# A fused attention and FP4 FFN layer on eight cores: own buffers for the first keys and values, another order of exponentials and statistics, x tiles ahead of the last chunks

## The chip, the cores and the metric

The kernel runs on the 8 cores of one Trainium2 chip. Each core takes two sequences of 2048 tokens out of sixteen and works alone; the weights are prepared on every core. The metric is the device time of the slowest core in microseconds. A core has TensorE (matmuls), VectorE, ScalarE, GpSimd (Pool) and SyncE (SP), each with its own instruction queue, done strictly in order; engines wait for each other through semaphores. DMAs are issued from the queues of ScalarE, Pool and SP.

## The reference

```python
xn = layernorm(x)                                  # rows of 1024
x = x + attention(xn) + ffn(xn)

# attention: 16 heads of 64, per sequence
q, k, v = split(xn @ Wqkv + bqkv)
# queries come in the order of a fixed mapping; every block of 64 queries
# sees 64 keys, each fourth of its segment of 256, also through the mapping
p = exp(q_block @ k_sel.T * D**-0.5 - rowmax)
out = (p @ v_sel) / (1e-6 + p.sum(-1)) @ Wproj + bproj

# ffn: weights [2816, 1024] twice and [1024, 2816]; xn, h and the weights go
# through fp4 (blocks of 16 along the last dimension, scale = max|.| / 6)
h = silu(fp4(xn) @ fp4(w_gate).T) * (fp4(xn) @ fp4(w_up).T)
ffn = fp4(h) @ fp4(w_down).T
```

## The kernel before

There are two blocks with a barrier between them. The first makes the attention part and, beside it, quantizes the FFN weights. The second is the FFN over 32 row tiles, and is not touched.

In the first block the FFN weights are cut into chunks of 128 rows: 24 of `wd` (stored to `wd_dram`), 22 of `wg`, 22 of `wu` (transposed by DMA into `wgqT` and `wuqT`), and two row tiles of x, which are normalized and quantized for the FFN. Each chunk c goes through a slot of VectorE (`slot(c)`: block maxima L746, scale and reciprocal L752 and L755, product L758; and for chunk c - 1 the rounding L749 and the last product L761) and a pass of ScalarE (`w_pass(c)`: L556 and L561, between the product and the rounding, then the load of chunk c + 2). SP stores or transposes the result (`w_store`). The buffers `wrow`, `wki` and `wcl` are double, so a chunk's load, pass and store each bound the chunk two further on.

`PRO` chunks belong to the prologue, which also loads the attention weights, gathers rows of x, makes the keys (`k_blocks`, four of two banks) and values (`v_rows`, four) of the first sequence, stores them to `k_dram` and `v_dram`, and makes the first queries. Keys go through one buffer `kst`, half of them at a time, and values through one buffer `vst`, a quarter at a time. Both alias or stand beside `wuqT`. The rows of x are handled in pieces of 128 rows: gathered by Pool into `lnx` (three buffers) or `lnk`, statistics by VectorE for two pieces at a time (`ln_batch`), normalized by ScalarE (`ln_apply`), turned by TensorE (`turn_piece`, L400) and copied out by ScalarE (`piece_evac`, L591).

Then there are 32 tiles J of 128 queries. `quota` says how many chunk slots a tile has, one or two; `TAIL` slots follow the last tile. In a tile TensorE turns the piece or pieces of `turned_at(J)`, projects the attention output of tile J - 2 (`proj`), makes the first half of the scores of J + 1, half a pair of queries (`q_half`), the second half of the scores, in tiles 5 to 12 a key or value block of the second sequence (`kv_at`), turns the output of J - 1, and multiplies with the values (`pv`). All results but scores and `pv` go through a ring of three PSUM banks `psR` in the order written out in `order`. VectorE takes the maxima of the scores (`colmax`, L786 and L791), does its slots and `norm(J - 1)` (L796 to L806). ScalarE makes the exponentials (`exps`, L645), copies out projections, queries, keys and values, the turned output (`at_evac`, L596), and does its passes.

Of VectorE's order in a tile before, these lines matter:

```python
colmax(J)
for i in batches_at(J): ln_batch(i)     # for turned_at(J + 1)
for c in slots[0:1]: slot(c)
if J >= 1: norm(J - 1)
for c in slots[1:]: slot(c)
```

## Time and profile before

| what | value |
|---|---|
| time, median of 3 runs | 1665.97 us (1660.42 to 1845.73) |
| profiled execution | 1663.18 us |
| its span, slowest core (core 5) | 1661.5 us |
| spans of the 8 cores | 1646.2 to 1661.5 us |
| busy of the span: TensorE, VectorE, ScalarE, Pool | 85%, 78%, 57%, 11% |
| mean granted clock of TensorE, core 5 | 0.928 of full |

The rows further below are of core 5, times in us from its first instruction. An idle time in square brackets is that of the engine just before the instruction, with what ended it. L numbers are lines of the kernel before. The first block ends near 735 us.

### The profile page before, as it was taken

How to read it: one execution, taken by the hardware profiler on the slowest of the kernel's cores; microseconds unless marked ns; L12 is line 12 of the kernel's file. 1: busy time of each engine (PE TensorE's matmuls, PEld its weight loads, DVE VectorE, ACT ScalarE, POOL GpSimd, SP SyncE). 2: the span in 40 equal slices, each digit the busy share in tenths (PEclk: the TensorE clock that was granted, in tenths of full speed). 3: DMA queues.
4: the chain of work that ended last, by engine and by line, in shares of the span. 5: the costliest groups of instructions: out<-in, count | busy, mean ns of one | idle time of the engine just before them, and what ended most of it. 6: DMA issues, size and time to landing. Idle time of an engine off the chain costs nothing.

```text
span 1661.5 us, 27839 instructions; the slowest of 8 cores (1646.2 to 1661.5 us)
## 1 busy us (share of the span) xinstructions
PE 1405.2 (85%) x8976; PEld 731.0 (44%) x8976; DVE 1287.9 (78%) x2251; ACT 941.1 (57%) x1594; POOL 181.9 (11%) x202
## 2 busy tenths in 40 slices
PE   0455788887777678649999999999999999999997
PEld 0224454454444445314444444444444444444443
DVE  3538876667877888848988888888888888888855
ACT  1436886677767777535555555545455555555542
POOL 4112212221221212000000000000000000000000
PEclk9978788999787778779999999999999999999999
DMA  7985455565777669884445454555555454545353
GB/s 157 212 215 175 142 152 156 166 157 169 184 163 188 170 149 180 177 184 93 92 120 121 102 105 108 108 108 109 115 106 119 96 128 97 103 110 111 90 105 90
DMA packets 252784, 225.68 MB, mean 136 GB/s; under 512 B 202914, under 2 KB 208034, under 8 KB 252642
## 3 DMA queue, kind: packets, MB, share of 16 engines
q1 hardware_dynamic: 213026, 103.91, 28.3%
q0 software_dynamic: 19616, 63.33, 18.4%
q10 hardware_dynamic: 20000, 56.66, 11.4%
q8 instruction: 74, 1.21, 0.3%
q14 instruction: 68, 0.56, 0.1%
HBM read 139.68 MB, written 43.81 MB: 110 GB/s over the span
## 4 chain that ended last, share of the span: by engine, by line
PE 52%; DVE 1%; DMA 1%; issue 1%; ACT 0%; DVEq 0%; SPq 0%; ACTq 0%
PE psD L1000 18%; PE psG L978 17%; PE psV L985 17%; DMA hqT<-wc 1%; DMA xb<-xin 0%; DVE sg L1081 0%; DVE wc L1102 0%; DVE am L1086 0%; DVE rs L1096 0%; DVE st_bn L122 0%; ACT xb L1041 0%; DVE xam L1064 0%; DVE st_bn L123 0%; DVE st_u L137 0%; DVE st_u L135 0%
## 5 line engine op out<-in xcount | busy, mean ns | idle before, releaser
L978 PE MATMUL psG<-wgqT,xq 128*128 128x512 bf16 (+1 forms) x1536 | 337.2, 363 | 17.4 <-PEq L268 17.4
L985 PE MATMUL psV<-wuqT,xq 128*128 128x512 bf16 (+1 forms) x1536 | 335.8, 362 | 0.0
L1000 PE MATMUL psD<-wdqT,hqT 128*128 128x512 bf16 x1408 | 316.7, 381 | 4.7 <-DMA hqT<-wc 4.7
L978 PEld LDWEIGHTS psG<-wgqT,xq 128*128 128x128 bf16 x1536 | 150.6, 98 | 178.8 <-issue 19.3
L985 PEld LDWEIGHTS psV<-wuqT,xq 128*128 128x128 bf16 x1536 | 150.4, 98 | 154.4 <-issue 0.8
L1000 PEld LDWEIGHTS psD<-wdqT,hqT 128*128 128x128 bf16 x1408 | 138.3, 98 | 166.8 <-issue 9.1
L1036 ACT COPY su<-psV 128x512 f32<-128x512 f32 (+1 forms) x192 | 105.7, 551 | 181.3 <-PE psV L985 181.2
L1032 ACT ACTIVATE sg<-psG 128x512 f32<-128x512 f32 (+1 forms) x192 | 107.8, 561 | 172.3 <-PE psG L978 172.2
L491 PE MATMUL psR<-wdqT,atT 128*128 128x512 bf16 x512 | 164.0, 478 | 11.9 <-ACT atT L596 11.8
L400 PE MATMUL psR<-ident,wdqT 128*128 128x128 bf16 x320 | 35.6, 281 | 154.0 <-ACT wdqT L572 95.0
L962 POOL DMA_DIRECT2D pp<-xin x32 | 28.0, 874 | 952.6 <-DMA pp<-partial_dram 952.3
L444 PE MATMUL psR<-wdqT 128*128 128x256 bf16 x1024 | 121.1, 278 | 7.6 <-ACT QT L635 3.0
L1014 ACT ACTIVATE ki<-sg 128x1408 int16<-128x1408 f32 x64 | 87.9, 1373 | 69.8 <-DVE sg L1099 69.8
L645 ACT ACTIVATE E<-psS,nb 128x64 bf16<-128x64 f32 x512 | 108.3, 370 | 2.4 <-DVE nb L791 2.4
L444 PEld LDWEIGHTS psR<-wdqT 128*128 128x128 bf16 x1024 | 99.4, 100 | 22.4 <-issue 8.4
L1099 DVE TENSOR_TENSOR sg<-sg,rs 128x1408 f32<-128x1408 f32 x64 | 104.0, 1625 | 6.7
L1086 DVE TENSOR_REDUCE am<-sg 128x88 f32<-128x1408 f32 x64 | 103.7, 1620 | 6.6
L1081 DVE TENSOR_TENSOR sg<-sg,su 128x1408 f32<-128x1408 f32 x64 | 103.8, 1622 | 2.5 <-ACT su L1036 1.7
L746 DVE TENSOR_REDUCE wam<-wrow 128x64 f32<-128x1024 f32 (+1 forms) x70 | 83.0, 1186 | 28.4 <-DMA wrow<-wd 21.6
L1102 DVE TENSOR_TENSOR wc<-wc,hsc 128x1408 bf16<-128x1408 f16 x64 | 103.5, 1618 | 0.1
L556 ACT ACTIVATE wki<-wrow 128x1024 int16<-128x1024 f32 (+1 forms) x70 | 72.3, 1034 | 54.2 <-DVE wrow L758 39.8
L749 DVE TENSOR_SCALAR wcl<-wcl 128x1024 uint16<-128x1024 uint16 (+1 forms) x70 | 29.1, 415 | 92.6 <-ACT wcl L561 92.3
(108 smaller groups left out, 1855.8 us busy)
## 6 DMA issues: line engine op xcount, KB each, us to landing
partial_dram<-po ACTq DMA_DIRECT2D x32, 512.0 KB
pp<-partial_dram SPq DMA_DIRECT2D x32, 512.0 KB, 4.7
pp<-xin POOLq DMA_DIRECT2D x32, 512.0 KB, 5.7
out<-pp SPq DMA_DIRECT2D x32, 512.0 KB, 5.4
xb<-xin SPq DMA_DIRECT2D x30, 512.0 KB, 5.2
wrow<-wg ACTq DMA_DIRECT2D x22, 512.0 KB
wrow<-wu ACTq DMA_DIRECT2D x22, 512.0 KB
wrow<-wd ACTq DMA_DIRECT2D x16, 512.0 KB
```

Of the source, the lines that this page charges most:

```text
L444: mm = tensor.matmul(ps[:, 256 * a:256 * (a + 1)], Wq[:, k, 128 * (2 * b + a):128 * (2 * b + a + 1)], src[:, k, :], start=(k == 0), stop=( ...
L491: tensor.matmul(ps[:], atT[:, k, :], Wproj_sb[:, k, 512 * oc:512 * (oc + 1)], start=(k == 0), stop=False)
L645: ev = scal.activation(E[J % 2][:, 64 * h:64 * (h + 1)], psS[:, 64 * h:64 * (h + 1)], AF.Exp, scale=SCALE, bias=nb_s[J % 2][:, h:h + 1])
L978: m = tensor.matmul(psG[g % 3][:, 0:iw], xqT[t % 2][:, k, :], wgqT[:, k, HU * half + i0:HU * half + i0 + iw], start=(k == 0), stop=(k == N ...
L985: m = tensor.matmul(psV[g % 3][:, 0:iw], xqT[t % 2][:, k, :], wuqT[:, k, HU * half + i0:HU * half + i0 + iw], start=(k == 0), stop=(k == N ...
L1000: m = tensor.matmul(psD[oc][:], hqT[u % 3][:, k, :], wdqT[:, HB * half + k, 512 * oc:512 * (oc + 1)], start=(half == 0 and k == 0), stop=( ...
L1032: silu_ev.inc(scal.activation(sg[s % 2][:, i0:i0 + iw], psG[g % 3][:, 0:iw], AF.Silu))
L1036: copy_ev.inc(scal.copy(su[s % 2][:, i0:i0 + iw], psV[g % 3][:, 0:iw]))
L1081: h_mul.inc(vec.tensor_mul(h, h, su[u % 2][:]))
L1086: h_am.inc(vec.tensor_reduce(am[u % 2][:], blocks(h), AX.X, ALU.max, apply_absolute_value=True))
L1099: h_v.inc(vec.tensor_tensor(blocks(h), blocks(h), spread(rs[u % 2][:], NB), ALU.mult))
L1102: h_out.inc(vec.tensor_tensor(blocks(w), blocks(w.bitcast(F16)), spread(sc[b % 2][:], NB), ALU.mult))
```

## The change

- `kst0` and `vst0`, in parts of `wgqT` that no chunk has reached yet, hold all keys and all values of the first sequence. Its keys are stored in one DMA of 1 MB after the fourth key block, in place of two halves; its four value blocks wait for no store. The second sequence has the small buffers as before. The counts of `kvst` follow, and SP waits for the first sequence's stores before the first gate chunk.
- ScalarE's prologue: passes 4 to 11 come earlier among the key, value and query copies; passes 12 to 14 are added. `PRO` is 15 in place of 12; tiles 14, 16 and 18 have one slot in place of two.
- ScalarE's tile begins with `exps(J)`; then the pieces are copied out, then the first pass, then `proj_evac`, and `ln_apply` for the next tile's pieces stands right behind it in place of at the tile's end.
- VectorE's statistics for `turned_at(J + 2)` stand at the end of tile J; before, those for `turned_at(J + 1)` stood behind `colmax(J)`. The batch of `turned_at(1)` goes into the prologue.
- The two x tiles are chunks 63 and 64, ahead of the last five of `wu`; they were the last two. Their statistics are called from within `slot`. With them the early transposes for `wdqT` begin one tile sooner (two in each of tiles 29, 30 and 31, then one behind each of two tail slots).

```diff
+        kst0 = normed[:, 8192:12288].rearrange("p (s a k) -> p s a k", a=8, k=64)
+        vst0 = normed[:, 12288:12288 + 4 * VW].rearrange("p (g h c) -> p g h c", g=4, c=65)
...
-            FIRST_GATE, FIRST_UP, FIRST_X = 3 * NKC, 3 * NKC + NIC, 3 * NKC + 2 * NIC
-            for r in range(2):
-                chunks.append((xin, xqT[r][:, :, :], r, 0, D))
+            FIRST_GATE, FIRST_UP = 3 * NKC, 3 * NKC + NIC
+            FIRST_X = FIRST_UP + NIC - 5
+            chunks[FIRST_X:FIRST_X] = [(xin, xqT[r][:, :, :], r, 0, D) for r in range(2)]
-            PRO = 12
+            PRO = 15
-            quota = [1 if J in (1, 2, 3, 4, 6, 8, 10, 12) else 2 for J in range(NJ)]
+            quota = [1 if J in (1, 2, 3, 4, 6, 8, 10, 12, 14, 16, 18) else 2 for J in range(NJ)]
...
                         if c == FIRST_GATE:
                             sync.wait_ge(ln_xn.h, kpiece(1, 3) + 1)
+                            sync.wait_ge(kvst.h, 16 * 5)
...
-                        if J >= NJ - 2:
-                            for r in range(2 * (J - NJ + 2), 2 * (J - NJ + 3)):
+                        if J >= NJ - 3:
+                            for r in range(2 * (J - NJ + 3), 2 * (J - NJ + 4)):
                                 wd_early(r)
...
                     def k_evac(q, b):
-                        if b % 2 == 0 and 6 * q + b // 2:
-                            scal.wait_ge(kvst.h, 16 * (6 * q + b // 2))
+                        if q == 1 and b == 2:
+                            scal.wait_ge(kvst.h, 16 * 6)
...
+                        if q == 0 and b == 3:
+                            scal.wait_ge(r_free.h, n + 2)
+                            scal.dma_start(out=k_dram[0][:, :].rearrange("(s p) c -> p s c", p=128),
+                                           in_=kst0.rearrange("p s a k -> p s (a k)")).then_inc(kvst.h, 16)
...
                     k_evac(0, 0)
+                    w_pass(4)
                     k_evac(0, 1)
-                    w_pass(4)
                     k_evac(0, 2)
+                    w_pass(5)
                     k_evac(0, 3)
-                    w_pass(5)
                     piece_evac(qpiece(0))
                     piece_evac(qpiece(1))
                     ln_apply(qpiece(2))
                     ln_apply(qpiece(3))
+                    w_pass(6)
                     v_evac(0, 0)
                     v_evac(0, 1)
-                    w_pass(6)
+                    w_pass(7)
                     v_evac(0, 2)
                     v_evac(0, 3)
-                    w_pass(7)
+                    w_pass(8)
...
                     for J in range(NJ + 2):
                         slots = slots_of(J)
+                        if J < NJ:
+                            exps(J)
                         for key in turned_at(J):
                             piece_evac(pieces.index(key))
-                        if J < NJ:
-                            exps(J)
+                        for c in slots[0:1]:
+                            w_pass(c)
                         if 0 <= J - 2 < NJ - 1:
                             proj_evac(J - 2)
-                        for c in slots[0:1]:
-                            w_pass(c)
+                        for key in turned_at(J + 1):
+                            ln_apply(pieces.index(key))
...
-                        for key in turned_at(J + 1):
-                            ln_apply(pieces.index(key))
...
-                            if c >= FIRST_X:
+                            if FIRST_X <= c < FIRST_X + 2:
+                                x_stats(c)
                                 vec.wait_ge(w_n.h, c - FIRST_X + 1)
...
+                    for i in batches_at(1):
+                        ln_batch(i)
                     for J in range(NJ + 1):
                         slots = slots_of(J)
                         if J < NJ:
                             colmax(J)
-                        for i in batches_at(J):
-                            ln_batch(i)
                         for c in slots[0:1]:
                             slot(c)
                         if J >= 1:
                             norm(J - 1)
                         for c in slots[1:]:
                             slot(c)
+                        for i in batches_at(J + 2):
+                            ln_batch(i)
```

`batches_at(J)` is now written for `turned_at(J)`. `w_pass(c)` ends, as before, with the load of chunk c + 2 and, ahead of an x tile, with its normalization (`x_norm(c + 1)`), which waits for VectorE's statistics.

## Rows read from the trace of the kernel before

**Rows 1.** Windows by stage: length, busy us (instructions) by engine, TensorE's clock, DMA share, GB/s.

```profile
0.00:151.40 151.40, 54.67 (x344) 29.74 (x344) 74.37 (x170) 56.84 (x71) 44.81 (x60) 0.93 0.85 198
...
227.10:374.70 147.60, 125.59 (x1159) 73.98 (x1156) 96.78 (x209) 104.74 (x240) 32.18 (x32) 0.91 0.57 156
374.70:486.65 111.95, 82.49 (x838) 51.28 (x836) 87.81 (x174) 80.22 (x178) 23.85 (x24) 0.85 0.67 175
486.65:612.60 125.95, 92.21 (x910) 57.12 (x910) 100.16 (x196) 91.92 (x204) 26.29 (x27) 0.78 0.68 168
612.60:702.20 89.60, 68.38 (x622) 38.61 (x623) 76.48 (x134) 64.55 (x154) 11.66 (x12) 0.77 0.85 178
...
735.00:1661.50 926.50, 917.38 (x4480) 439.25 (x4480) 772.00 (x1172) 472.26 (x603) 27.96 (x32) 0.99 0.50 108
```

**Rows 2.** Waits of VectorE, 152 to 728 us: total, times, longest.

```profile
DVE wcl L749 <- ACT wcl L561: 63.3, 15, 8.8
DVE mx L786 <- PE psS L465: 14.5, 7, 3.6
```

**Rows 3.** Timeline of VectorE, tiles 19 and 20.

```profile
486.65 1.22 DVE L786 TENSOR_REDUCE mx<-psS 128x16 f32<-128x1024 f32 x1
...
492.85 0.29 DVE L796 TENSOR_SCALAR ls<-psP 128x6 f32<-128x6 f32 x3
...
495.12 1.21 DVE L746 TENSOR_REDUCE wam<-wrow 128x64 f32<-128x1024 f32 x1
500.64 0.43 DVE L749 TENSOR_SCALAR wcl<-wcl 128x1024 uint16<-128x1024 uint16 x1 [4.31 <-ACT wcl L561]
...
504.20 1.22 DVE L786 TENSOR_REDUCE mx<-psS 128x16 f32<-128x1024 f32 x1
...
523.38 1.22 DVE L786 TENSOR_REDUCE mx<-psS 128x16 f32<-128x1024 f32 x1
```

**Rows 4.** Timeline of ScalarE, tile 19.

```profile
487.87 1.23 ACT L572 ACTIVATE wdqT<-lnx,row_n,row_r 128x1024 bf16<-128x1024 f32 x1
490.45 1.01 ACT L591 COPY wdqT<-psR 128x1024 bf16<-128x1024 bf16 x1 [1.36 <-PE psR L400]
491.36 3.38 ACT L645 ACTIVATE E<-psS,nb 128x64 bf16<-128x64 f32 x16
...
499.48 1.06 ACT L561 ACTIVATE wcl<-wki 128x1024 f16<-128x1024 int16 x1
```

**Rows 5.** Timeline of ScalarE in the prologue.

```profile
78.59 0.39 ACTq L610 DMA_DIRECT2D k_dram<-wuqT  x1
...
100.25 1.84 ACT L605 ACTIVATE wuqT<-psR,bqk 128x512 bf16<-128x512 f32 x3 [18.90 <-DMA k_dram<-wuqT]
```

**Rows 6.** DMA queues (packets, MB, share), 85 to 90 us, then 104 to 108.

```profile
q0 software_dynamic: 362, 0.66, 87.8%
q10 hardware_dynamic: 364, 0.19, 17.3%
...
q0 software_dynamic: 218, 0.76, 49.5%
```

**Rows 7.** Timeline of VectorE in the prologue.

```profile
103.39 1.22 DVE L746 TENSOR_REDUCE wam<-wrow 128x64 f32<-128x1024 f32 x1 [12.78 <-DMA wrow<-wd]
...
140.66 1.22 DVE L746 TENSOR_REDUCE wam<-wrow 128x64 f32<-128x1024 f32 x1 [1.73 <-DMA wrow<-wd]
...
151.36 1.22 DVE L786 TENSOR_REDUCE mx<-psS 128x16 f32<-128x1024 f32 x1
```

**Rows 8.** Timeline of VectorE, tiles 7 and 8.

```profile
279.25 0.43 DVE L749 TENSOR_SCALAR wcl<-wcl 128x1024 uint16<-128x1024 uint16 x1 [8.83 <-ACT wcl L561]
...
298.56 1.23 DVE L786 TENSOR_REDUCE mx<-psS 128x16 f32<-128x1024 f32 x1 [1.95 <-PE psS L465]
```

**Rows 9.** The tail: timeline of VectorE, then of SP's queue.

```profile
726.81 1.22 DVE L761 TENSOR_TENSOR wcl<-wcl,wsc 128x1024 bf16<-128x1024 f16 x1
...
730.81 1.36 SPq L285 DMA_TRANSPOSE xq<-wcl x1
```

More of the change, by code:

```diff
@@ L97, in build_nc @@
         kxT = early[:, 16384:20480].rearrange("p (k t) -> p k t", t=512)
-        kst = early[:, 20480:22528].rearrange("p (s a k) -> p s a k", a=4, k=64)
+        kst1 = early[:, 20480:22528].rearrange("p (s a k) -> p s a k", a=4, k=64)
         normed = wgqT[:].rearrange("p k n -> p (k n)")
+        kst0 = normed[:, 8192:12288].rearrange("p (s a k) -> p s a k", a=8, k=64)
+        vst0 = normed[:, 12288:12288 + 4 * VW].rearrange("p (g h c) -> p g h c", g=4, c=65)
         lnk = [normed[:, 2048 * i:2048 * (i + 1)].bitcast(F32) for i in range(4)]
@@ L311, in _ @@
                         if i < 2:
-                            wd_early(4 + 2 * i)
-                            wd_early(5 + 2 * i)
+                            wd_early(6 + i)
                     sync.wait_ge(wdl_early.h, 16 * NKC)
@@ L337, in gather_kv @@
                         if j == 0:
-                            gpsimd.wait_ge(kvst.h, 16 * 6 * (q + 1))
+                            gpsimd.wait_ge(kvst.h, 16 * (5 + 6 * q))
                         if J >= 3:
@@ L366, in _ @@
                     gpsimd.memset(vst[:, :, 64:65], 1.0).then_inc(ones_done.h, 1)
+                    gpsimd.memset(vst0[:, :, :, 64:65], 1.0).then_inc(ones_done.h, 1)
                     for n in range(3, 5):
@@ L564, in w_pass @@
                             w_load(c + 2)
-                        if FIRST_X <= c + 1 < NCH:
+                        if FIRST_X <= c + 1 < FIRST_X + 2:
                             x_norm(c + 1)
@@ L615, in v_evac @@
                         if q == 0 and g == 0:
-                            scal.wait_ge(ones_done.h, 1)
-                        else:
-                            scal.wait_ge(kvst.h, 16 * (6 * q + 2 + g) if g else 16 * 6)
+                            scal.wait_ge(ones_done.h, 2)
+                        if q == 1 and g >= 1:
+                            scal.wait_ge(kvst.h, 16 * (5 + 2 + g))
+                        dst = vst0[:, g] if q == 0 else vst[:]
                         for oc in range(2):
                             scal.wait_ge(r_full.h, n + oc + 1)
-                            scal.copy(vst[:, 8 * oc:8 * (oc + 1), 0:64],
+                            scal.copy(dst[:, 8 * oc:8 * (oc + 1), 0:64],
                                       psR[(n + oc) % 3][:].rearrange("p (h d) -> p h d", d=64)).then_inc(r_free.h, 1)
@@ L691, in _ @@
                     ln_apply(qpiece(5))
-                    w_pass(8)
+                    w_pass(9)
                     q_evac(0, 0)
-                    w_pass(9)
+                    w_pass(10)
                     q_evac(0, 1)
-                    w_pass(10)
+                    w_pass(11)
                     q_evac(1, 0)
                     piece_evac(qpiece(4))
-                    w_pass(11)
+                    for c in range(12, PRO):
+                        w_pass(c)
                     for J in range(NJ + 2):
                         slots = slots_of(J)
+                        if J < NJ:
+                            exps(J)
                         for key in turned_at(J):
                             piece_evac(pieces.index(key))
-                        if J < NJ:
-                            exps(J)
+                        for c in slots[0:1]:
+                            w_pass(c)
                         if 0 <= J - 2 < NJ - 1:
                             proj_evac(J - 2)
-                        for c in slots[0:1]:
-                            w_pass(c)
+                        for key in turned_at(J + 1):
+                            ln_apply(pieces.index(key))
                         if q_step(J)[0] < NJ // 2:
@@ L780, in x_stats @@
                         xs_nm.inc(row_stats(vec, [wrow[c % 2][:]], 3, row_r[:, r:r + 1], row_n[:, r:r + 1]))
-                    batches_at = lambda J: [m // 2 for m in map(pieces.index, turned_at(J + 1)) if m % 2 == 0]
+                    batches_at = lambda J: [m // 2 for m in map(pieces.index, turned_at(J)) if m % 2 == 0]
                     def colmax(J):
```

15 lines of the change are left out of this document (7 added, 8 removed).

## The prediction

> **What bounds the kernel now.** I read the windows by stage first [rows 1]. From 735 us on the FFN runs with TensorE busy 917 of 926.5 us, and nothing of the change is in that block, so those 926.5 us stay. The 735 us before it are where the change acts, and no engine is full there: VectorE is the nearest. So I read what VectorE waits for [rows 2]: in the tile loop it stands 63.3 us, 15 times, before the rounding step on `wcl` (L749) because ScalarE has not made `wcl` yet, and 14.5 us, 7 times, before colmax for the scores. Then I read one pair of tiles in order of time [rows 3]. Tile 20 (504.20 to 523.38) takes 19.18 us with no wait: it has two chunk slots and a batch of row statistics. Tile 19 (486.65 to 504.20) has two slots, no batch, takes 17.55 us and holds a wait of 4.31 us. So its work is 13.24 us, the batch costs 19.18 - 13.24 = 5.9, and from the rows inside tile 19 (495.12 to 504.20 less 4.31) one slot costs 4.8, norm 2.3. The reason of the wait stands in ScalarE's rows of tile 19 [rows 4]: it normalizes the piece at 487.87, waits for TensorE to turn it, copies it out at 490.45, only then begins the exponentials (491.36), and the first chunk's pass ends at 500.5; the pass was computable long before. In the prologue the same reading gives one large hole: ScalarE stands 18.90 us before the third key block for the store of the first [rows 5], and VectorE 12.78 us for chunk 6 [rows 7]. The tail is VectorE's last product, then SP issuing the last transpose at 730.81 [rows 9].
>
> **The prologue.** Own buffers `kst0` and `vst0` remove the 18.90 us wait and the one for the vector store behind it. What is late next? ScalarE now meets `w_pass(6)` ahead of the value blocks, and that needs chunk 6. Its load was queued behind the key store on ScalarE's ring. In 85 to 90 us that ring and the software queue each got through some 70 packets per us, 364 against 362 [rows 6]: one for one. The store is 1024 packets, so it took its 21 us because of their number. After the change the loads of chunks 6 and 7 (128 packets each) are issued before the store (all eight blocks must be copied first, I work out 86 us), so chunk 6 lands near 85, not 103.4; then the store's 1024 packets of twice the size take 15 to 20 us and hold back chunk 8 to about 104. VectorE's batch 4 then needs a row gather that Pool issues once ScalarE has normalized piece 2 (near 92, before 111); it stands in the software queue, which is running out at 104 to 108 [rows 6]: I take 108. From there VectorE has batch 4 (5.9), seven slots (8 to 14, before four) at the 5.35 us a slot of the last two before (140.66 to 151.36 [rows 7]), which already holds the waits for loads, and batch 5, which stood behind colmax before: 108 + 5.9 + 37.5 + 5.9 = 157.3 against 151.4. So tile 0 begins 6 us later, with three chunks and a batch more behind it: 20 us of VectorE work for 6. Bounds: -2 (the gather lands at 100) and +12 (chunk 6 lands no earlier than before, so slot 8 starts near 120). I take +6, since the packet rows are of this very queue. The one more memset on Pool is under 1 us in a queue that waits for loads anyway.
>
> The Trainium skill (DMA: Bandwidth & Descriptors, "Queues, rings and completion order") says that each DMA engine takes turns between its rings a packet at a time; the 364 to 362 agree, and by it chunk 6 lands early. The same page ("Issuing engines are not separate DMA queues") speaks against a gain: all queues share the same 16 engines. By that alone chunk 6 would come when the software queue empties; that is the +12 end, and the first rival.
>
> **Tiles 0 to 4** (75.7 us, between the first two stages [rows 1]). The batch of tile J now stands at the end of J - 1, ahead of the next colmax; four batches lie here, before five: -5.9. Tile 4 is then short of VectorE work and goes by ScalarE and the scores: +3.7 from the colmax waits, which run from 0.2 to 3.6 us [rows 2]. Sum -2 (bounds -6, +3).
>
> **Tiles 5 to 12** (147.6 us, 18.45 a tile). Here the second sequence's keys and values are made. VectorE is busy 96.8 us of them, so the batch is covered; the 8.83 us wait [rows 8] is ScalarE's lateness again. TensorE has 125.6 us, 15.7 a tile [rows 1], ScalarE 13.1. In the new order TensorE turns the piece and projects while ScalarE still does the previous tile, the copy follows the exponentials without the 1.36 us wait [rows 4]. What is late next is the ring of three banks: q's second bank needs the first projection copied out. I give 1.4 us a tile for that on top of TensorE's 15.7: 17.1 x 8 = 137, -11. Bounds: 15.9 a tile (-20), and 18.45 (0).
>
> **Tiles 13 to 18** (112.0 us). Quota is now one slot in 14, 16 and 18. VectorE's pair was 13.24 + 19.18 = 32.4, now less one slot 27.6. In the one-slot tile colmax comes early and waits for scores: I add 2.6 (2.1 on average [rows 2]). ScalarE: exponentials 3.15, copy 0.9, pass 2.2 after nb; VectorE needs the pass 9 us after nb (slot 4.8, norm 2.3, half a reduce), so the 4 us wait is gone with 2 us to spare. 3 x 30.2 = 90.7, +3 for matmuls at the lower clock (granted 0.85 here): 94, -18. Bounds -24 (27.6 a pair and the clock kept) and -10 (half the wait stays).
>
> **Tiles 19 to 25** (126.0 us). Same chunks as before; only the waits go. Three pairs at 32.4 and one tile of 13.24: 110.5. Where no batch stands between two slots, a load has some 7 us from issue to need, and the DMA engines are 0.68 busy: I add 3 for that. 113.5, -12. Bounds -15 and -3 (the waits stay, as loads).
>
> **Tiles 26 to 31 and the tail** (122.4 us to 735). One wait of this kind falls away (-3). The two x tiles go from the tail into tiles 29 and 30, with their statistics, ScalarE's normalization and the wait for it: the same VectorE work. ScalarE stands in `x_norm` behind `w_pass(62)` and `w_pass(63)` until VectorE has come to the statistics; queued behind are `proj_evac`, `at_evac` and once `exps(30)`; VectorE needs none of them before its next two slots, so this costs nothing here, and up to 5 if it does. The tail is now three plain slots, but with DMA 0.85 busy the loads get no pause: +6. SP's last transpose no longer stands behind two early ones for `wd` (728.03 to 730.81 [rows 9]): -3. Those early transposes start one tile sooner, behind conditions that hold by tile 29. Sum 0 (bounds -8, +8).
>
> **The sum.** +6 - 2 - 11 - 18 - 12 + 0 = -37. The profiled execution took 1663.2 us (span 1661.5 and 1.7 around it), so 1626; the median of the runs stands 2.8 us above it, and I predict 1628 us, 2.3% under 1666. A measurement of this kernel tells about 2% from no change, that is 1633: the forecast is near that edge.
>
> **Rivals.** (1) DMA takes the bound. For: 0.85 busy in 612 to 702, and 0.67 to 0.68 in 375 to 612 with less done per us than wanted now; VectorE's waits turn from ScalarE into loads and `wcl` transposes. Against: only two load waits in the loop, both late. Price: the prologue at +12, and 2 us in each of the 14 tiles 13 to 26, which is half the gain: -37 + 6 + 20 = -11, 1655.
> (2) The store wait was worth all of its 19 us: the gather lands by 100 and colmax(0) is at 149, and tiles 5 to 12 go at TensorE's own 15.9: -37 - 8 - 9 = -54, 1611. For: the engines were idle, not busy, at 85 to 100. Against: seven chunk slots are a chain of loads that nothing shortens.
> (3) The other side: TensorE becomes the bound at its lower clock. It has two levels, 1.2 and 2.4 GHz, and was granted 0.91 in tiles 5 to 12 and 0.78 to 0.85 behind them [rows 1]. The new order makes it wait for the exponentials between projection and scores, in the middle of its work. A tile of 5 to 12 needs about 16 us at full clock, the others 11.7. If 0.91 fell to 0.70, the eight tiles would take 22.9 each, +35 in place of -11, and the others 16.7 for 16.2, +10: -37 + 46 + 10 = +19, 1685. It decides from a mean grant below 0.75 there. Against: total idle of TensorE shrinks as the tiles shorten.
> (4) The change does less than it says: the order frees ScalarE, but the late pass is only exchanged for a late projection copy and late scores: half of tiles 13 to 25: -37 + 15 = -22, 1644.
>
> **Chances.** Forecast 0.50 (own range 1615 to 1640; 0.37 of it under 1633), (1) 0.18, (2) 0.13, (3) 0.08, (4) 0.11. Faster by over 2%: 0.37 + 0.13 = 0.50; slower by over 2%, that is past 1699: 0.03 of (3) and 0.03 of (1), where both grow past what I price: 0.06; within: 0.44. The range for 8 in 10 reaches from (2)'s upper half to (1): 1608 to 1656.
>
> **What would show it.** Right: no wait of ScalarE for `k_dram`; chunk 6 landed by 90; colmax(0) at 152 to 163; the L749 waits in the loop from 63 to under 15 us; pairs near 32.4 us in 19 to 24 and 30 in 13 to 18; no projection or turn of TensorE behind `ln_apply`. Wrong: if colmax(0) is past 165, if VectorE waits for `wrow` or ScalarE for transposes of `wcl` over 20 us in the loop, or if the granted clock in tiles 5 to 12 is under 0.8.

## The result, and the profile after

| | median of the runs | ratio to before |
|---|---|---|
| before | 1665.97 us | |
| after | 1639.71 us (4 runs, 1636.45 to 1783.88 us) | 0.9852, 95% interval 0.9804 to 0.9901 |
| forecast | 1628 us (1608 to 1656) | 0.977 |

The kernel is faster by 1.5%, within the 2% that a measurement of it can tell from no change. The profiled execution took 1640.51 us, 22.7 us less than before's, and the slowest core is now core 3 with a span of 1638.7 us. Runs in which the cores of one die ran at a lower clock count in the medians of this table and are left out of every ratio and of the medians further below; without them the two medians are 1663.20 and 1638.91 us.

The windows by stage of core 3 of the kernel after, to be held against [rows 1]; columns are start and end, length, busy us (instructions) of TensorE, its weight loads, VectorE, ScalarE and Pool, then TensorE's granted clock, DMA share and GB/s:

```profile
0.00:174.25 174.25, 58.92 (x344) 31.52 (x344) 91.94 (x203) 64.01 (x78) 42.58 (x61) 0.85 0.80 190
...
252.43:382.27 129.84, 117.87 (x1159) 70.32 (x1157) 97.77 (x209) 102.93 (x237) 30.24 (x31) 0.99 0.61 178
382.27:481.64 99.37, 78.86 (x814) 49.98 (x813) 74.28 (x157) 73.91 (x174) 24.77 (x25) 0.88 0.72 174
481.64:592.40 110.76, 84.43 (x938) 55.10 (x935) 99.92 (x195) 88.58 (x202) 26.07 (x25) 0.91 0.68 184
592.40:682.00 89.60, 60.21 (x580) 34.56 (x576) 76.79 (x153) 63.92 (x153) 13.51 (x12) 0.81 0.76 169
...
708.93:1638.70 929.77, 918.84 (x4480) 439.54 (x4480) 772.59 (x1172) 473.12 (x603) 27.69 (x32) 0.99 0.50 108
```

The windows are the prologue, tiles 5 to 12, 13 to 18, 19 to 25, the 89.6 us from tile 26 on (as in [rows 1]) and the FFN. The first has grown from 151.4 to 174.25 us; tiles 5 to 12, 13 to 18 and 19 to 25 take 129.84, 99.37 and 110.76 us in place of 147.60, 111.95 and 125.95. Since the slowest core is another one than before, I took the stages of all eight cores from the timelines (the first colmax, the colmax of tiles 5, 13, 19 and 26, the first matmul of the FFN) and use their means from here on:

| stage, mean of 8 cores, us | before | after | difference | forecast |
|---|---|---|---|---|
| prologue, to colmax(0) | 149.6 | 172.0 | +22.4 | +6 |
| tiles 0 to 4 | 75.4 | 75.7 | +0.3 | -2 |
| tiles 5 to 12 | 146.8 | 130.0 | -16.8 | -11 |
| tiles 13 to 18 | 110.5 | 97.9 | -12.6 | -18 |
| tiles 19 to 25 | 124.5 | 110.2 | -14.3 | -12 |
| tile 26 to the FFN | 120.2 | 115.6 | -4.6 | 0 |
| first block | 727.0 | 701.3 | -25.7 | -37 |

From tile 0 on the loop gave 48 us where 43 were forecast. The prologue took 22 back where 6 were forecast, and that is the miss. The FFN, which the change does not touch, took 927.8 us in the mean of the cores and 925.9 before.

**The prologue.** VectorE's timeline of the kernel after, core 3 (compare [rows 7]; the third batch of statistics, the fourth, and the first colmax):

```profile
85.75 0.70 DVE L124 BATCH_NORM_STATS2 st_bn<-xq 128x6 f32<-128x512 f32 x1 [4.06 <-DMA lnx<-xin,qidx]
...
122.56 0.70 DVE L124 BATCH_NORM_STATS2 st_bn<-lnx 128x6 f32<-128x512 f32 x1 [21.60 <-DMA xq<-xin,qidx]
...
174.25 1.23 DVE L798 TENSOR_REDUCE mx<-psS 128x16 f32<-128x1024 f32 x1
```

The same batch in VectorE's timeline of the kernel before, core 5:

```profile
124.96 0.69 DVE L122 BATCH_NORM_STATS2 st_bn<-lnx 128x6 f32<-128x512 f32 x1
```

Batch 4 waits 21.60 us for a gather and starts at 122.56; before it started at 124.96, with no wait ahead of it. Removing ScalarE's 18.90 us wait [rows 5] moved that batch by 2.4 us (from 123.7 to 122.0 in the mean of the eight cores). Pool's timeline of the kernel after, core 3, shows why:

```profile
76.32 4.36 POOL L373 DMA_DIRECT2D wdqT<-Wproj  x8
...
85.28 0.94 POOL L328 DMA_INDIRECT wgqT<-xin,kidx  x1 [0.27 <-issue]
93.60 0.93 POOL L334 DMA_INDIRECT xq<-xin,qidx  x1 [7.38 <-ACT wdqT L575]
...
136.70 0.94 POOL L334 DMA_INDIRECT lnx<-xin,qidx  x1 [40.96 <-ACT wdqT L575]
```

And Pool's timeline of the kernel before, core 5:

```profile
111.28 0.94 POOL L332 DMA_INDIRECT xq<-xin,qidx  x1 [24.10 <-ACT wdqT L572]
```

The gather is issued at 93.60, before at 111.28: 18 us earlier, as the change intends. But it lands at 122. It stands in the software queue behind the eight loads of `Wproj` and four gathers of keys, and that queue is served more slowly while ScalarE's ring has packets. The DMA queues of the kernel after, core 3 (packets, MB, share), 100 to 105 us, then 120 to 125:

```profile
q0 software_dynamic: 352, 0.98, 74.4%
q10 hardware_dynamic: 355, 0.36, 21.3%
...
q10 hardware_dynamic: 310, 0.70, 35.5%
q0 software_dynamic: 63, 0.21, 10.3%
```

352 packets of the one for 355 of the other. Before, ScalarE waited for the first key store until 99.74 us on this core, had put nothing behind it but one load, and issued the next store only at 105.00; so its ring was nearly empty from 100 to 105. The same window of core 3 before:

```profile
q0 software_dynamic: 458, 1.61, 86.3%
q10 hardware_dynamic: 40, 0.11, 8.0%
```

1.61 MB of the software queue against 0.98. From 85 to 100 the two queues had gone one for one before too; it is above all the ring left empty at the end of the wait that let the software queue run out. From 80 to 105 us that queue moved 4.23 MB before and 3.30 after, and 0.63 of the 0.93 MB between them belong to these 5 us. After 105 it had 0.22 MB left before, and after the change 2.35, of which the two gathers are 1.05 (2 x 128 rows of 4 KB). Nor is a gather done when the backlog is: before, with the queue empty, the same one took 5.2 us from its issue to its landing (core 3).

**The loop.** VectorE's waits from 176 to 705 us on core 3 of the kernel after, to be held against [rows 2] (total, times, longest):

```profile
DVE mx L798 <- PE psS L468: 37.5, 9, 8.1
DVE wcl L761 <- ACT wcl L564: 18.1, 10, 3.1
```

The wait for ScalarE's pass fell from 63.3 us (core 5) to 18.1 (core 3) and 20.7 (core 5). The wait of colmax for the scores rose from 14.5 to 37.5 and 29.2. VectorE's timeline in tiles 14 to 17, then in tiles 20 to 22 (compare [rows 3]):

```profile
404.83 1.22 DVE L798 TENSOR_REDUCE mx<-psS 128x16 f32<-128x1024 f32 x1
...
417.25 1.23 DVE L798 TENSOR_REDUCE mx<-psS 128x16 f32<-128x1024 f32 x1 [3.85 <-PE psS L468]
...
436.48 1.22 DVE L798 TENSOR_REDUCE mx<-psS 128x16 f32<-128x1024 f32 x1
...
449.74 1.23 DVE L798 TENSOR_REDUCE mx<-psS 128x16 f32<-128x1024 f32 x1 [4.69 <-PE psS L468]
...
500.44 1.23 DVE L798 TENSOR_REDUCE mx<-psS 128x16 f32<-128x1024 f32 x1
...
513.61 1.22 DVE L798 TENSOR_REDUCE mx<-psS 128x16 f32<-128x1024 f32 x1
...
533.22 1.23 DVE L798 TENSOR_REDUCE mx<-psS 128x16 f32<-128x1024 f32 x1
```

Tiles 20 and 21 take 533.22 - 500.44 = 32.8 us with no wait ahead of a colmax, against the 32.4 worked out. Tiles 14 and 16, with one slot, end in waits of 3.85 and 4.69 us: a slot that is taken out there is mostly waited out.

**The tail.** VectorE's timeline, then SP's queue, of the kernel after on core 3, compare [rows 9]:

```profile
703.66 0.43 DVE L761 TENSOR_SCALAR wcl<-wcl 128x1024 uint16<-128x1024 uint16 x1 [2.97 <-ACT wcl L564]
704.20 1.23 DVE L773 TENSOR_TENSOR wcl<-wcl,wsc 128x1024 bf16<-128x1024 f16 x1
...
705.49 1.22 SPq L288 DMA_TRANSPOSE wuqT<-wcl  x1
```

SP issues the last transpose 0.06 us after the last product has ended (704.20 + 1.23 = 705.43); before, 2.8 us after.

### The profile page after: what moved, and what is told of

Its sections match the earlier page's. It is cut to its first block, busy times and chain, and to the rows that moved or that the text cites. A ratio compares the mean times of both kernels' runs of the same rounds, so it can differ in the third digit from the quotient of the medians.

```text
span 1638.7 us, 27833 instructions; the slowest of 8 cores (1617.1 to 1638.7 us)
## 1 busy us (share of the span) xinstructions
PE 1390.1 (85%) x8976; PEld 725.3 (44%) x8976; DVE 1288.3 (79%) x2251; ACT 936.9 (57%) x1594; POOL 182.4 (11%) x203
## 4 chain that ended last, share of the span: by engine, by line
PE 53%; SPq 1%; DVE 1%; DMA 1%; issue 1%; DVEq 0%; ACT 0%; ACTq 0%
PE psD L1012 18%; PE psG L990 17%; PE psV L997 17%; SPq L952 1%; DMA hqT<-wc 0%; DMA xb<-xin 0%; DVE sg L1093 0%; DVE wc L1114 0%; DVE rs L1108 0%; DVE am L1098 0%; SPq L932 0%; DVE st_bn L124 0%; DVE pp L1064 0%; DVE st_bn L125 0%; DVEq L928 0%
## 5 line engine op out<-in xcount | busy, mean ns | idle before, releaser
L447 PE MATMUL psR<-wdqT 128*128 128x256 bf16 x1024 | 146.3, 308 | 66.0 <-ACT wdqT L594 46.7
L447 PEld LDWEIGHTS psR<-wdqT 128*128 128x128 bf16 x1024 | 109.0, 110 | 97.1 <-issue 73.1
L494 PE MATMUL psR<-wdqT,atT 128*128 128x512 bf16 x512 | 130.5, 401 | 16.8 <-ACT atT L599 9.1
L1111 DVE TENSOR_TENSOR sg<-sg,rs 128x1408 f32<-128x1408 f32 x64 | 104.1, 1626 | 6.7
L559 ACT ACTIVATE wki<-wrow 128x1024 int16<-128x1024 f32 (+1 forms) x70 | 76.4, 1092 | 39.2 <-DVE wrow L770 35.7
L1034 ACT ACTIVATE wc<-ki 128x1408 f16<-128x1408 int16 x64 | 87.6, 1369 | 5.2 <-ACT ki L1026 0.4
L770 DVE TENSOR_TENSOR wrow<-wrow,wrs 128x1024 f32<-128x1024 f32 (+1 forms) x70 | 83.7, 1196 | 7.7 <-DVE wrs L767 0.5
```

Of the source, the lines that this page charges most:

```text
L447: mm = tensor.matmul(ps[:, 256 * a:256 * (a + 1)], Wq[:, k, 128 * (2 * b + a):128 * (2 * b + a + 1)], src[:, k, :], start=(k == 0), stop=( ...
L494: tensor.matmul(ps[:], atT[:, k, :], Wproj_sb[:, k, 512 * oc:512 * (oc + 1)], start=(k == 0), stop=False)
L1111: h_v.inc(vec.tensor_tensor(blocks(h), blocks(h), spread(rs[u % 2][:], NB), ALU.mult))
```

## The experiments

Each puts one part of the change (or two) on the kernel before, or changes one to three things in the kernel after. Stages are means over the 8 cores, in us, read as in the table above.

| kernel | median us | ratio, 95% | colmax(0) | 0 to 4 | 5 to 12 | 13 to 18 | 19 to 25 | 26 to FFN |
|---|---|---|---|---|---|---|---|---|
| e1_loop_only | 1624.85 | 0.9739, 0.9690 to 0.9789 | 155.4 | 74.7 | 130.8 | 100.6 | 111.1 | 116.9 |
| e2_prologue_only | 1670.16 | 1.0012, 0.9975 to 1.0049 | 164.7 | 75.9 | 147.7 | 99.8 | 124.7 | 118.9 |
| e3_gather_first | 1637.65 | 0.9801, 0.9739 to 0.9864 | 162.8 | 76.1 | 130.5 | 98.8 | 110.4 | 119.4 |
| e4_two_k_stores | 1649.71, one run | | 173.0 | 75.0 | 130.7 | 98.1 | 110.7 | 117.6 |
| e5_pro12 | 1632.69 | 0.9811, 0.9771 to 0.9851 | 154.6 | 76.0 | 130.6 | 100.7 | 111.3 | 118.2 |
| e6_pro12_gather_first | 1619.11 | 0.9709, 0.9665 to 0.9753 | 146.0 | 75.7 | 131.0 | 100.7 | 111.2 | 117.1 |
| e7_scalar_order_only | 1621.27 | 0.9737, 0.9692 to 0.9782 | 150.4 | 79.3 | 127.1 | 100.6 | 111.0 | 116.2 |
| e8_vector_order_only | 1663.14 | 0.9990, 0.9966 to 1.0013 | 157.4 | 69.8 | 147.0 | 110.5 | 123.9 | 119.2 |
| e9_gather_first_vector_old | 1621.18 | 0.9736, 0.9712 to 0.9760 | 145.2 | 79.0 | 127.1 | 101.9 | 111.4 | 117.1 |
| e10_own_buffers_vector_old | 1625.78 | 0.9764, 0.9733 to 0.9795 | 153.0 | 79.1 | 127.0 | 100.8 | 111.2 | 115.0 |
| e11_scalar_order_early_x | 1629.92 and 1623.01 | | 153.8 | 79.6 | 127.3 | 100.8 | 111.2 | 117.4 |
| e12_scalar_order_gather_first | 1621.27 | 0.9750, 0.9722 to 0.9778 | 151.8 | 79.5 | 127.0 | 101.9 | 110.9 | 116.0 |

### e1_loop_only: the tile order of both engines on the kernel before

```diff
 # ScalarE, tile J
+                        if J < NJ:
+                            exps(J)
                         for key in turned_at(J):
                             piece_evac(pieces.index(key))
-                        if J < NJ:
-                            exps(J)
...
 # VectorE: ln_batch of turned_at(1) ahead of tile 0, of turned_at(J + 2) at the end of tile J
```

> The kernel before with only the new order inside the tiles (exponentials first, statistics at the end of a tile and two tiles ahead, one batch before tile 0); prologue, buffers, quota, chunks and x tiles as before. Theory: all of the gain comes from here. Tile 0 begins one batch (5.9 us) later than before, near 155.5 (mean of the cores), and from there to the FFN it takes 577 - 48 + 14 = 543 us, since the three slots of tiles 14, 16 and 18 are in the loop again. FFN at 699 and about 1637 us, ratio 0.983, as good as the whole change. Rival: the loop is shorter mainly because three slots and a batch were taken out of it; then it is here about 577 - 20 - 8 = 560 us and the ratio 0.993.

It gave 0.9739, more than either theory expected and more than the whole change. With the old prologue the loop takes 534.1 us from colmax(0) to the FFN (529.4 after, 577.4 before). So the prologue of the change costs more than its shorter quota returns.

### e2_prologue_only: own buffers, new prologue order, PRO 15 and the shorter quota, with the old tile order and the x tiles last

```diff
-            PRO = 12
+            PRO = 15
-            quota = [1 if J in (1, 2, 3, 4, 6, 8, 10, 12) else 2 for J in range(NJ)]
+            quota = [1 if J in (1, 2, 3, 4, 6, 8, 10, 12, 14, 16, 18) else 2 for J in range(NJ)]
...
+                        if q == 0 and b == 3:
+                            scal.dma_start(out=k_dram[0][:, :].rearrange("(s p) c -> p s c", p=128),
```

> The change without the new order in the tiles and with the x tiles at the end: own buffers, new order of the prologue, PRO 15, quota. Theory: tile 0 begins at 172 - 6 = 166 us, 16 later than before; in the loop three slots of 4.7 us are gone, 14 us at most, so the whole is 1.00 to 1.01. Rival (the buffers and the earlier chunks pay, the loop order is a small thing): under 0.99.

1.0012: nothing. The prologue is 15.1 us longer, tiles 13 to 18 are 10.7 shorter. With the old order a slot less in tiles 14, 16 and 18 is worth 3.6 us each; with the new order (after against e1) it is worth 2.7 us for the three. The two parts of the change do not add, and VectorE's waits in tiles 13 to 18 (summed from the timelines, mean of the 8 cores) say why. Here the wait for ScalarE's pass is 16.0 us (before 13.4): it stays, and each slot taken out saves most of its work. In the kernel after the pass wait is 3.1, but colmax waits 11.6 for the scores (e1 0.3): a slot taken out is waited out.

### e3_gather_first: the kernel after, with the gathers of pieces 5 and 6 ahead of `Wproj` and the key gathers in Pool's queue

```diff
+                    for n in range(5, 7):
+                        gather_q(n)
                     for k in range(NKC):
                         gpsimd.dma_start(out=Wproj_sb[:, k, :], ...)
...
-                    for n in range(5, 8):
+                    for n in range(7, 8):
                         gather_q(n)
```

> The changed kernel, but Pool issues the gathers of pieces 5 and 6 before the loads of Wproj and the four gathers of key rows, not after them. Theory: batch 4 waits (20 to 22 us in the trace) because the gather of piece 5 lies in the software queue behind 2 x 4 MB of other traffic, which takes turns with ScalarE's ring; with nothing ahead of it it lands near 102 instead of 122, batch 4 begins there, slots 8 to 14 run at 5.4 each, tile 0 begins near 152 to 156 in place of 172; 1622 us, ratio 0.974. Rival: tile 0 is late by three slots and one batch (22 us) because the slots are a chain of loads and passes; then it stays at 168 to 172 and the ratio at 0.985.

VectorE's timeline on core 4 of this kernel: the first instruction of batch 4, then the waits behind it.

```profile
100.95 0.69 DVE L124 BATCH_NORM_STATS2 st_bn<-lnx 128x6 f32<-128x512 f32 x1
...
116.12 1.22 DVE L760 TENSOR_REDUCE wam<-wrow 128x64 f32<-128x1024 f32 x1 [5.50 <-DMA wrow<-wd]
124.79 1.22 DVE L760 TENSOR_REDUCE wam<-wrow 128x64 f32<-128x1024 f32 x1 [4.22 <-issue]
133.19 0.95 DVE L760 TENSOR_REDUCE wam<-wrow 128x48 f32<-128x768 f32 x1 [3.62 <-DMA wrow<-wd]
143.44 1.22 DVE L760 TENSOR_REDUCE wam<-wrow 128x64 f32<-128x1024 f32 x1 [6.11 <-DMA wrow<-wd]
```

The gather wait is gone and batch 4 starts 22 us earlier (99.7 for 122.0 in the mean), so the place in the software queue was its cause. But tile 0 came only 9 us earlier, not the 16 to 20 expected. The next slots stand 19.5 us before a chunk's block maxima: 5.50 + 3.62 + 6.11 for chunk loads, and 4.22 for which the trace names no releaser. From batch 4 to colmax(0) it is now 63.1 us. So the gather was only the last of the late transfers; that they are all late because they share the DMA engines is likely, and not shown apart. Nearly 6 of the 9 us are lost again behind tile 0 (535.2 us to the FFN, 529.4 after), and the whole, 0.9801, is not told apart from the kernel after (the intervals overlap).

### e4_two_k_stores: the kernel after, its key store made twice

```diff
+                            scal.dma_start(out=k_dram[1][:, :].rearrange("(s p) c -> p s c", p=128),
+                                           in_=kst0.rearrange("p s a k -> p s (a k)")).then_inc(kx2.h, 16)
```

The second sequence's keys wait for that store and overwrite it later.

> The changed kernel with the first sequence's key store issued twice on ScalarE's ring, the second time into the other sequence's buffer in DRAM, which is overwritten later (results as before). 1024 packets more. If rings take turns packet by packet, the 1024 packets delay the software queue's by as many: the gather of piece 5 lands about 10 to 15 us later (near 134) and tile 0 begins there, near 184. If only the bytes count (1 MB at 220 GB/s), 5 us: tile 0 near 177. If the gather does not set tile 0, it stays at 172.

Neither delay came: colmax(0) stayed at 173.0 (172.0 without), and batch 4 began at 123.45 behind 19.58 us of wait for the gather (core 4), so the gather was not late either. That is the number of the third branch, but not its reason. The ring was never empty between 96 and 124 us in the kernel after, so the added packets only lengthened ScalarE's own queue and took no more turns from the software queue. So this run tests neither branch: that the ring's packets slow the software queue is read from the packet counts of both kernels, and no run took packets off the ring while the queue had its backlog. What the added packets did was hold ScalarE: issuing one load, elsewhere some 0.3 us, took 12.35 (ScalarE's queue, core 4 of this kernel).

```profile
99.13 12.35 ACTq L547 DMA_DIRECT2D wrow<-wd  x1
```

### e5_pro12 and e6_pro12_gather_first: the kernels after and e3 with PRO 12 and the old quota

```diff
-            PRO = 15
+            PRO = 12
-            quota = [1 if J in (1, 2, 3, 4, 6, 8, 10, 12, 14, 16, 18) else 2 for J in range(NJ)]
+            quota = [1 if J in (1, 2, 3, 4, 6, 8, 10, 12) else 2 for J in range(NJ)]
```

> The whole change but with PRO 12 and the quota of before: own buffers, new prologue order, new tile order, early x tiles. Theory (three prologue slots cost their full 16 us because the prologue is a chain, and give back only 2.7 us in tiles 13 to 18): tile 0 begins near 172 - 16 = 156, the loop takes 529 + 3 = 532, FFN at 688 to 690, 1626 us, ratio 0.974, equal to the kernel with the tile order alone (0.9739). Rival (the three slots fill idle time in the prologue, since VectorE waits 20 us there for a gather): tile 0 stays past 165 and the ratio stays near 0.985.

> As the run before, with the gathers of pieces 5 and 6 ahead of the Wproj loads and the key gathers. Theory: gather order and slot chain add up: tile 0 at 156 - 9 = 147, FFN at 679, 1617 us, ratio 0.968. Rival: with twelve prologue chunks the first queries or the key and value gathers for tile 0 (they need piece 4) become the late thing, and tile 0 stays at 152 or later; 1622 us or more.

e5 came out at 0.9811 where 0.974 was expected; its interval does not reach there. Its stages say what the three slots are worth: 172.0 - 154.6 = 17.4 us in the prologue, 5.8 a slot, against 100.7 - 97.9 = 2.8 in tiles 13 to 18. In e5 batch 4 still starts at 124.14 behind a wait of 21.29 us (core 0). e6 does what was expected, 0.9709 and colmax(0) at 146.0: the early gather is worth 8.6 us here too (9.2 with 15 chunks).

### e7_scalar_order_only and e8_vector_order_only: each engine's tile order alone on the kernel before

```diff
 # e7: ScalarE, tile J
+                        if J < NJ:
+                            exps(J)
                         for key in turned_at(J):
                             piece_evac(pieces.index(key))
-                        if J < NJ:
-                            exps(J)
+                        for c in slots[0:1]:
+                            w_pass(c)
                         if 0 <= J - 2 < NJ - 1:
                             proj_evac(J - 2)
-                        for c in slots[0:1]:
-                            w_pass(c)
+                        for key in turned_at(J + 1):
+                            ln_apply(pieces.index(key))
...
-                        for key in turned_at(J + 1):
-                            ln_apply(pieces.index(key))
 # e8: VectorE only, ln_batch as in e1
```

> The kernel before with only ScalarE's new order in a tile (exponentials first, ln_apply behind the projection copy); VectorE's statistics stay right behind colmax, for one tile ahead. Theory: the 63 us of waits at L749 were made by ScalarE's order alone. Tile 0 at 149.6 as before, the loop 535 to 545 in place of 577, FFN at 685 to 695, ratio 0.972 to 0.979. Rival: both moves are needed, since ln_apply in the middle of a tile now meets statistics that are only just made; then 560 and more, 0.99.

> The kernel before with only VectorE's new order (statistics at the end of a tile, two tiles ahead); ScalarE as before. Theory: the L749 waits stay, the batch only changes sides of colmax; tile 0 at 155.5, the loop 570 to 583, ratio 0.998 to 1.007. Rival (VectorE's move is what matters): 0.985 or less.

Both as the theory had it: 0.9737 and 0.9990. The whole gain of the change is in the order of ScalarE. VectorE's waits from 156 to 700 us, core 1 of e7:

```profile
DVE wcl L749 <- ACT wcl L561: 18.0, 12, 3.1
DVE mx L786 <- PE psS L465: 17.8, 9, 3.0
```

The pass wait is at the value of the whole change, 18.0 us for 18.1. e8's tile order takes 69.8 us in tiles 0 to 4 in place of 75.4, and gives it back ahead of them (157.4 in place of 149.6): a batch is moved, and a moved batch saves nothing.

### e9 to e12: what is left of the other parts

e9 is e6, and e10 is e5, with VectorE's statistics in the old place. e11 is e7 with the x tiles ahead of the last five chunks. e12 is e7 with the two gathers first in Pool's queue.

```diff
 # e9, e10
-                    for i in batches_at(1):
-                        ln_batch(i)
...
                             colmax(J)
+                        for i in batches_at(J):
+                            ln_batch(i)
...
-                        for i in batches_at(J + 2):
-                            ln_batch(i)
 # e11
+            FIRST_X = FIRST_UP + NIC - 5
+            chunks[FIRST_X:FIRST_X] = [(xin, xqT[r][:, :, :], r, 0, D) for r in range(2)]
 # e12: the same lines as e3
```

> PRO 12 with own buffers, ScalarE's new order, x tiles early and the two gathers first (1620.0 us), with VectorE's statistics back in the old place. Theory (a batch of statistics ahead of tile 0 is paid in the prologue, 5.9 us, and its place in the loop is worth nothing): tile 0 at 140 to 142 us in place of 146.0, the loop from tile 0 to the FFN 534 to 537 as with ScalarE's order alone (534.2), so 1614 us, ratio 0.969. Rival (chunk loads set the end of the prologue, since VectorE waits 13.5 us for them behind that batch, so the batch fills a wait): tile 0 stays at 145 to 147, 1620 us, ratio 0.972.

> The kernel of the change with PRO 12 and the old quota, and VectorE's statistics in the old place: own buffers, ScalarE's new order and the early x tiles, the gathers where they were. Theory (the late gather holds tile 0 through batch 4, which now stands behind tile 0): tile 0 at 147 to 149 us, 1622 us, ratio 0.973. Rival (own buffers bring a gain of their own, 19 us of ScalarE's wait, once nothing waits for the gather): tile 0 at 140 or before, ratio 0.967. Second rival (loads of chunks are what is late, with or without the gather): tile 0 at 150 to 155, ratio 0.976 or more.

> The kernel before with ScalarE's new order (1621.6 us, 0.9737) and the x tiles ahead of the last five chunks, nothing else. Theory (the move of the x tiles is worth -2 to +2 us): 0.9725 to 0.975, the stretch from tile 26 to the FFN 114 to 118 us (116.2 without). Rival (it shortens the tail as two transposes fewer stand before the last one): 112 us or less, 0.971. Other rival (ScalarE stands in the x tiles' normalization with exponentials behind it): 121 us or more, 0.977.

> The kernel before with ScalarE's new order, and the two gathers ahead of the projection weights and the second sequence's key rows; no own buffers, so ScalarE still waits 18 us for the key store. Theory (own buffers and the early gathers work only together: without own buffers piece 2 is normalized at 111 us and the gathers cannot be issued earlier): tile 0 at 149 to 152 as without (150.4), ratio 0.974; the weights that now stand behind the gathers are not needed before tile 2. Rival (the early gathers are the whole of the 8.6 us that they brought with own buffers): tile 0 at 142, ratio 0.969.

e9 went to its rival: colmax(0) at 145.2, 1621.18 us. But the batch did not fill a wait for loads, as that rival had it: without it VectorE waits for the scores, 5.7 to 13.7 us on the eight cores, here core 1 of e9:

```profile
148.04 1.23 DVE L800 TENSOR_REDUCE mx<-psS 128x16 f32<-128x1024 f32 x1 [10.99 <-PE psS L470]
```

e10 came out at 153.0 and 0.9764. It has the late gather in batch 4 (core 2: 124.38 behind 23.04 us of wait): batch 4 stands ahead of tile 0 in both orders, the one that VectorE's new order adds ahead of tile 0 is batch 5, and its expectation mixed them up. The number falls under its second rival, though on four cores colmax(0) stands 6.0 to 8.8 us for the scores and not for a load. e11 has only the two times of the table, too few for a ratio; its last stage, 117.4 against e7's 116.2, shows no gain from the x tiles. Its colmax(0) at 153.8 against e7's 150.4, with the same prologue, suggests that colmax(0) moves by some 3 us from one execution to the next; smaller differences of it are not told apart.

e12 is the most telling. Its time is e7's (1621.27 us both), as its theory had it, but not for the theory's reason: ScalarE does not wait 18 us for the key store any more, and the gathers are issued at 97.55, not at 111. ScalarE's timeline, and the DMA queues from 80 to 85 us, core 1 of e12:

```profile
79.35 0.39 ACTq L612 DMA_DIRECT2D k_dram<-wuqT  x1
...
86.75 1.84 ACT L607 ACTIVATE wuqT<-psR,bqk 128x512 bf16<-128x512 f32 x3 [4.64 <-DMA k_dram<-wuqT]
...
122.91 1.08 ACT L623 CAST vst<-psR 128x512 bf16<-128x512 f32 x2 [8.02 <-DMA v_dram<-vst]
...
q10 hardware_dynamic: 1078, 0.86, 60.6%
q0 software_dynamic: 163, 0.55, 29.8%
```

Pool stands before the gathers, so `Wproj` is issued 22 us later (99.69 us, in e7 77.39) and the software queue runs out; the same store of 512 KB then lands within 7.4 us (79.35 to 86.75) in place of 21.7 [rows 5]. So an exchange of issues on another queue takes most of the wait for the key store away without own buffers. But ScalarE then stands 6.02 + 5.07 + 8.02 = 19.1 us for the value stores through the one buffer `vst` (7.5 in e7, same core), which `vst0` would remove: the wait has moved on. colmax(0) does not come earlier: VectorE's slots wait for a load (7.14 us at 137.27) and stand 8.64 and 7.92 us before the rounding step (108.84 and 126.85), the latter for ScalarE's pass, which stands behind the 8.02 us.

Own buffers by themselves are e10 against e11 (153.0 and 153.8): nothing. Together with the early gathers they bring colmax(0) from 151.8 (e12) to 145.2 (e9), and the mean of the cores' spans is 5.0 us shorter (1608.4 and 1613.4), but the slowest core is not (1619.7 and 1619.4), and the slowest core is the metric.

## Why the prediction missed its number

**The step that failed: "+6" for the prologue, and in it "I take 108" and the 5.35 us a slot behind it.** The prediction read that the software queue was running out at 104 to 108 [rows 6] and let the gather, once issued, land then. It landed at 122. The queue ran out at that time with the help of a ring that ScalarE's wait had left empty from 100 to 105; the change removes that very wait, and fills the ring: the key store of 1024 packets at 89.27 us, then two loads and four value stores between 96.22 and 109.39. The prediction had the rule for it, one for one, applied it to the ring (when does chunk 6 land?) and not to the queue on the other side (what do these packets cost the backlog that the gather stands behind?). It also gave the gather no time of its own. Behind that point the sum looks right: from batch 4 to colmax(0) it gave 157.3 - 108 = 49.3 us, measured 174.25 - 122.56 = 51.7. But that is luck in part. e3 has batch 4 at 99.7, earlier than the 108, and colmax(0) at 162.8 all the same: 63.1 us in between, 15.2 of them waits for chunk loads on core 4. A gather at 108 would hardly have done better. So of the 16 us that were missed the gather's lateness explains some 9 (e3), and an estimate of 7 is left for the slots, whose "5.35 us a slot" was to hold the waits for loads already and did not. The bound of +12, which supposed that chunk 6 would be late, was not wide enough either, since another transfer was late.

**20 us of VectorE work for 6.** This was the exchange that the prologue was to give. The work is there (5.8 us a slot in e5, and 1 to 8 us for batch 5: e9 to e6 0.8, e10 to e5 1.6, e7 to e1 5.0, before to e8 7.8), and nothing hid it, as batch 4 began where it began before.

**Tiles 0 to 4, -2.** +0.3, within its bounds. The batch is out (e8: -5.6), and ScalarE's order costs 3.9 here (e7).

**Tiles 5 to 12, -11.** -16.8: 130.0 us or 16.3 a tile, near the 15.9 of the bound and of rival 2. TensorE is busy 117.87 of 129.84 us on core 3, at a granted clock of 0.99 in place of 0.91. Its idle time, charged with 1.4 us a tile, is (129.84 - 117.87) / 8 = 1.5; what the sum missed is that its busy time fell from 15.7 to 14.7 a tile with the clock. e7 alone gives -19.7, so the mechanism, the order of ScalarE, is shown.

**Tiles 13 to 18, -18.** -12.6. The wait was removed as worked out (e7: -9.9 with two slots everywhere), but "3 x 30.2" took a whole slot of 4.8 us out of each pair and gave 2.6 back; colmax then waited 3.85 to 4.69 us in place of 2.1, so the slot was worth 0.9 (2.7 us for the three, after against e1). The term of the sum was mis-sized by the wait of a one-slot tile.

**Tiles 19 to 25, -12.** -14.3. Pairs of 32 to 32.8 us for 32.4; the 3 us for loads were not needed: the largest load wait in the loop is 0.9 us.

**Tile 26 to the end, 0.** -4.6 in total, but e1, with the x tiles last, has 116.9 against 115.6: the move of the x tiles gives at most 1.3 (e11 against e7 has it cost 1.2), and the rest is ScalarE's order (e7: 116.2). ScalarE stood 5.66 and 5.46 us ahead of the x tiles' normalization (647.66 and 660.46 on core 3), and nothing queued behind it was missed, as argued.

**The signs named ahead.** Right: no wait for `k_dram`, pairs in 19 to 24, loads no bound in the loop, the granted clock not under 0.8 in 5 to 12. Chunk 6 had landed by 91.24, when its slot began without a wait. Missed by a little: L749 (now L761) at 18 to 21 us for under 15, and pairs of 31.7 and 31.9 us in 14 to 17 for 30. Wrong: colmax(0) at 168.6 to 175.2 on the eight cores, past the 165 that was named as the sign of failure.

**The rivals.** (3) is refuted: the granted clock rose from 0.91, 0.85 and 0.78 (core 5) to 0.99, 0.88 and 0.91 (core 3) in tiles 5 to 12, 13 to 18 and 19 to 25, while TensorE's idle time in them shrank from 22.0, 29.5 and 33.7 us to 12.0, 20.5 and 26.3. (4) gave the nearest number, 1644, by a mechanism that did not happen: tiles 19 to 25 lost nearly all of their wait for the pass (15.8 us on core 5 before, 1.2 on core 3 after). (1) was wrong in the loop and right in the prologue, beyond its price; that price was also summed wrongly, as 2 us in each of 14 tiles are 28 and not 20, which makes 1663 in place of 1655. (2) was nearly right in tiles 5 to 12 (16.3 us a tile for 15.9) and wrong in the prologue. The forecast's own last step is a slip of 1 us: 1626 and 2.8 make 1629, not 1628. The Trainium skill's sentence that all queues share the same engines (DMA: Bandwidth & Descriptors, "Issuing engines are not separate DMA queues") was given the +12 end and no more; here e3 and e12 agree with it: with the gathers brought forward, waits for chunk loads (e3) and for value stores (e12) came in their place.

**What is open.** Why e5 and e10, with the own buffers, come to 1632.69 and 1625.78 while e7 has 1621.27 is not settled: their first blocks end at 691.4, 686.2 and 684.6, and 4.2 and 2.6 us of that are colmax(0), about as much as it moves by itself. At 145 to 153 us TensorE makes the first queries with 1 to 2.7 us between its matmuls, busy 1.82 of the 8 us (after, core 3), and ScalarE stands 7.5 to 8.2 us before it copies them out, on some cores of after, e5 and e10; what holds them there was not tried. Of the versions that keep ScalarE's order and 12 chunks in the prologue only e5 is told apart from others, from e6 and e9; all other intervals overlap; e7 is the smallest edit, six moved lines, and e6 has the lowest ratio, 0.9709. Both beat the kernel after.

## What to carry to other kernels

The end of a long wait on one engine can be the time in which another queue empties. Before pricing a removed wait at its length, list what the engine will issue in its place, and who stands behind a shared backlog; here 18.90 us of wait brought the next milestone some 2 us forward. Try the reordering of an in-order engine alone before buffers and quotas are changed with it: here six moved lines held all of the gain, 0.0263 of the time, and the rest of the change gave 0.0115 of it back. Taking work off an engine pays only while that engine is what the next step waits for: a slot taken from a tile was worth 3.6 us before the reorder and 0.9 after it, when the scores came last.

## What the runs showed of the hardware

Two queues with packets outstanding were served one for one whatever their packets' size: 352 to 355 in 5 us while the software queue's were 2.8 KB on average and the ring's 1.0 KB. The key store of 512 KB in 1024 packets was done in 7.4 us where the software queue ran out (e12: 1078 packets of the ring in 5 us), and took 21.7 beside a full one (364 in 5 us [rows 6]): a factor of three. In the kernel before, the second store of the same size, issued at 105.00 as the software queue ran out, landed in 4.2 us (core 3). The Trainium skill states the turns (DMA: Bandwidth & Descriptors, "Queues, rings and completion order"); the trace agrees, and adds the price. And a DMA issue on ScalarE is not always short: behind two stores of some 1000 packets each on its ring one issue held the engine 12.35 us (e4).
